# First expert layer: the 26-row tail of the down product in fp32 on four column blocks, and W2's high part made on GpSimd

## The chip, the cores and the metric

The kernel runs on one core of one Trainium2 chip. The metric is device time in microseconds (us) of one launch; lower is better. Three runs of the kernel before took 1910.48, 1913.32 and 1914.53 us, a median of 1913.32 us.

The engines are named as in the profile: PE (TensorE matmuls) with PEld (its weight loads), DVE (VectorE), ACT (ScalarE), POOL (GpSimd) and SP (SyncE, which issues DMAs here).

## The reference, cut to what matters

The network has four attention layers and four feed-forward layers in turn. The change lies in the first feed-forward layer, a mixture of 8 experts, each token going to its two best, each expert taking at most C = 538 rows of 256 numbers:

```python
C = int(round(K * T * CAP_RATIO / E))                       # 538
h = gelu(einsum('ecd,edh->ech', buf, W1) + b1[:, None, :])  # 538 x 256 times 256 x 1024
y = einsum('ech,ehd->ecd', h, W2) + b2[:, None, :]          # 538 x 1024 times 1024 x 256
```

The second line of arithmetic is called the up product below, the third the down product. Both are to be had in about fp32 accuracy.

## The kernel before

The program is written engine by engine: each engine has one function per layer, its instructions run in the order in which they are written, and engines meet at semaphores alone (`wait_ge`, `then_inc`). No scheduler moves anything.

**Split operands.** A fast matmul form takes operands rounded to fewer bits ("rounded" in the profile, type fp32r). Each matrix is therefore split into a high part (a rounded copy, `act_hi`, `act_split_w1`, `act_split_w2`) and a low part (the rest, `dve_lo`, one SCALAR_TENSOR_TENSOR at L918), and a product is the sum of three matmuls: high by high, high by low, low by high.

**One expert.** For expert x, PE does (`pe_ffn0`):
- `pe_up0`: eight blocks f of 128 hidden units. A block is 12 matmuls of 270 columns (two halves of the 540 row slots), into banks 4 and 5 or 6 and 7 in turn. Before it writes a pair of banks again it waits for the Gelu of block f-2.
- `pe_rows` for expert x + 1: ten transposes that turn the next expert's rows, into banks 0, 1 and 2.
- `pe_down0`: five blocks a of rows, four of 128 and a tail of 26. A block is 24 matmuls of 256 columns (8 blocks f by three products), so the tail costs PE the same 24 matmuls as a full block. The blocks go to banks 3, 2, 3, 2, 3 in turn; block a waits for DVE to have taken block a-2 (`s_yd`), except that block 1 waits only for the tail of the turned rows to have left bank 2 (`s_xpd`).

**Around it, for each block f of the up product:** ACT does the Gelu (L1113, 128x540, out of PSUM into `f0_HF`, which has two buffers, so that Gelu f waits for the low part of f-2); the high part of h is made by ACT for even f (L1119) and by DVE for odd f (L1156, a CAST); DVE makes the low part (L918). Behind blocks 1 and 3 ACT makes one half of W2's high part (L915, 128x1024) and DVE the low part (L918, 128x1024).

**After the eighth block** ACT, then DVE, split the next expert's turned rows (three pieces) and its W1 (two halves). Only then does DVE's program come to `f0_Y = PSUM + b2` (L1173), which empties the five down blocks one by one. POOL waits for each and scatters its rows to memory (L1210, an indirect DMA), then makes the row indices of expert x + 2 (L1071).

**Loads.** SP loads the weights of expert x + 2, 2 MB in one DMA, as soon as expert x's W1 and W2 are split, into the buffer that they leave.

Of the kernel before, what the change touches and what calls it, by code (L numbers as in the profile page):

```python
# [92 lines left out]
def build(nc, d, out):  # L93
    with ExitStack() as ctx:
# [64 lines left out]
        s_zsrc, s_zero, s_w0 = sem("zero_tile"), sem("buffers_zeroed"), sems("ffn0_w_in", 2)  # L159
        s_gate, s_bf = sem("gates"), sem("bf16_consts")  # L160
        s_rin, s_rout = sems("rows_in", 4), sems("rows_out", 3)
        s_x, s_bn, s_rs, s_xn = sem("x_tile"), sem("bn_stats"), sem("rstd"), sem("xn_tile")
        s_tp, s_xt = sem("turned"), sem("xt_cols")

# [58 lines left out]
        def sp_begin(e):  # L223
            e.dma_start(X[:, 0:4, :], d["x"][:, 0:4, :]).then_inc(s_xin[0], 16)
            e.dma_start(view(oC, NCST), d["cst"]).then_inc(s_const, 16)
            e.dma_start(ctxT, d["ctxT"]).then_inc(s_const, 16)
            e.dma_start(view(oS, NSML), d["sml"]).then_inc(s_const, 16)
            e.dma_start(X[:, 4:8, :], d["x"][:, 4:8, :]).then_inc(s_xin[1], 16)
            e.dma_start(view(oAW, 2048), d["aw"][0]).then_inc(s_aw[0], 16)
            for g in range(2, 4):  # L230
                e.dma_start(X[:, 4 * g:4 * g + 4, :], d["x"][:, 4 * g:4 * g + 4, :]).then_inc(s_xin[g], 16)
            e.dma_start(view(oAW + 2048, 2048), d["aw"][1]).then_inc(s_aw[1], 16)
            for x in range(2):
                e.dma_start(view(oW + 4096 * x, 4096), d["w0"][x]).then_inc(s_w0[x], 16)
            sp_blank(e)
# [4 lines left out]
        def sp_blank(e):  # L240
            e.wait_ge(s_zsrc, 1)
# [10 lines left out]
        def pool_begin(e):  # L252
            e.memset(view(z_tile, RW), 0.0).then_inc(s_zsrc, 1)
            e.wait_ge(s_const, 48)
            for t in range(NT):
                pool_rstd(e, t + 1, t)
# [44 lines left out]
        s_kv, s_kb, s_vp, s_vz = sem("kv_prod"), sem("kb_ready"), sem("vp_ready"), sem("vp_blank")  # L301
# [76 lines left out]
        def dve_heads(e, L):  # L378
# [14 lines left out]
            e.wait_ge(s_vz, 2 * L + 2)  # L393
# [496 lines left out]
        XP, HP = rview(oXT, 2, 2, CAP + 2), rview(o + 4160, 2, 8, CAP + 2)  # L890
        f0_B2, f0_Y = view(oXT + 2160, 2, 256), view(oXT + 2672, 3, 256)
# [6 lines left out]
        s_xg = sem("rows_blank")  # L898
# [3 lines left out]
        s_dn, s_yd = sem("down_prod"), sem("y_ready")  # L902
        s_f0b = sems("b2_in", 2)
# [16 lines left out]
        def act_split_w1(e, x):  # L920
            e.wait_ge(s_w0[x % 2], 16 * (x // 2 + 1))
            if x:
                e.wait_ge(s_up, 8 * x)
            for k in range(2):
                act_hi(e, W1P[:, 0, k], raw_w1(x, k), s_w1a)

        def dve_split_w1(e, x):
            e.wait_ge(s_w0[x % 2], 16 * (x // 2 + 1))
# [6 lines left out]
        def act_split_w2(e, x, h):  # L935
            if x:
                e.wait_ge(s_dn, 5 * x)
            act_hi(e, parts_w2(h)[0], raw_w2(x, h), s_w2a)

# [12 lines left out]
        def pe_rows(e, x):  # L952
# [11 lines left out]
            if x >= 2:  # L964
                e.wait_ge(s_yd, 5 * (x - 1) - 1)
# [18 lines left out]
        def down_bank(a):  # L984

            return 3 - a % 2

        def pe_down0(e, x):
            e.wait_ge(s_w2d, 2 * x + 2)
            for a in range(5):  # L990
                n = 128 if a < 4 else 26
                bk = down_bank(a)
                if a >= 2:
                    e.wait_ge(s_yd, 5 * x + a - 1)
                elif a == 1 and x < 7:
                    e.wait_ge(s_xpd, 3 * x + 6)
                elif x:
                    e.wait_ge(s_yd, 5 * x - a)
                for f in range(8):
                    if a == 0:  # L1000
                        e.wait_ge(s_hl, 8 * x + f + 1)
                    for i, j in ((0, 0), (0, 1), (1, 0)):
                        m = mm(e, psum[0:n, bk, 0:256], HP[:, i, f, 128 * a:128 * a + n], W2P[:, j, f, :],
                               (f, i, j) == (0, 0, 0), (f, i, j) == (7, 1, 0))
                m.then_inc(s_dn, 1)

# [60 lines left out]
        def pool_ids0(e, x):  # L1067
            e.wait_ge(s_rin[x % 2], 32 * (x // 2 + 1))
            if x == 0:
                e.wait_ge(s_xg, 1)  # L1070
# [3 lines left out]
        def pe_ffn0(e):  # L1074
            pe_ranks0(e, 1)
            pe_ranks0(e, 2)
            pe_rows(e, 0)
# [18 lines left out]
        def act_ffn0(e):  # L1096
# [10 lines left out]
            for x in range(8):  # L1107
                for f in range(8):
                    bk, hf = 4 + 2 * (f % 2), f0_HF[:, f % 2, :]
                    e.wait_ge(s_up, 8 * x + f + 1)  # L1110
                    if 8 * x + f >= 2:
                        e.wait_ge(s_hl, 8 * x + f - 1)
                    e.activation(hf.rearrange("p (c n) -> p c n", c=2), psum[:, bk:bk + 2, 0:270], ACT.Gelu,  # L1113
# [6 lines left out]
                    if f in (1, 3) and x:  # L1120
                        act_split_w2(e, x, f // 2)
                if x < 7:
                    act_rows(e, x + 1)
                    act_split_w1(e, x + 1)

        def dve_ffn0(e):
# [15 lines left out]
            e.memset(f0_Xg[:, :, 4, :], 0.0).then_inc(s_xg, 1)  # L1142
# [53 lines left out]
        def pool_ffn0(e):  # L1196
# [10 lines left out]
            for x in range(8):  # L1207
                for a in range(5):
# [4 lines left out]
                    ny += 1  # L1213
                if x < 6:
                    pool_ids0(e, x + 2)
# [6 lines left out]
        def sp_ffn0(e):  # L1222
            def load_w(x):
                e.wait_ge(s_w1d, 2 * (x - 1))
                e.wait_ge(s_w2d, 2 * (x - 1))
                e.dma_start(view(oW + 4096 * (x % 2), 4096), d["w0"][x]).then_inc(s_w0[x % 2], 16)
# [18 lines left out]
            e.wait_ge(s_xg, 1)  # L1245
# [3 lines left out]
            for x in range(6):  # L1249
# [3 lines left out]
                load_b(x + 2)  # L1253
            e.wait_ge(s_dn, 40)
# [1888 lines left out]
```

## Time and profile before

| | us |
|---|---|
| median of three runs | 1913.32 |
| span of the profiled execution | 1915.2 |
| PE busy in the span | 1641.2 (86%) |
| DVE, ACT, POOL busy | 1092.3, 898.9, 837.6 |
| chain that ended last, PE's share | 64%, of it 60% at L166 |
| chain at L166 in one expert: 216 matmuls | 26.43 |

The page gives the profiled execution by its span alone, from the first instruction to the last; no other time is listed for it. It is 1.9 us over the median and 0.7 us over the slowest of the three runs. The expert stage of this layer lies between 170 and 397 us of the span. All matmuls are issued by one helper at L166, the low parts by another at L918, so that groups by line mix layers: rows are to be read by time and by shape.

### The profile page before, as it was taken

How to read it: one execution, taken by the hardware profiler on the slowest of the kernel's cores; microseconds unless marked ns; L12 is line 12 of the kernel's file. 1: busy time of each engine (PE TensorE's matmuls, PEld its weight loads, DVE VectorE, ACT ScalarE, POOL GpSimd, SP SyncE). 2: the span in 40 equal slices, each digit the busy share in tenths (PEclk: the TensorE clock that was granted, in tenths of full speed). 3: DMA queues.
4: the chain of work that ended last, by engine and by line, in shares of the span. 5: the costliest groups of instructions: out<-in, count | busy, mean ns of one | idle time of the engine just before them, and what ended most of it. 6: DMA issues, size and time to landing. Idle time of an engine off the chain costs nothing.

```text
span 1915.2 us, 26188 instructions
## 1 busy us (share of the span) xinstructions
PE 1641.2 (86%) x9225; PEld 1117.0 (58%) x9225; DVE 1092.3 (57%) x2218; ACT 898.9 (47%) x1454; POOL 837.6 (44%) x754
## 2 busy tenths in 40 slices
PE   5954999969966999965996887999999999997998
PEld 3444999946844333355993665555555654563674
DVE  4762556576967355532446798565656666644335
ACT  2322445513335897823443664555454355431363
POOL 3053211123479454422005464566656666754206
PEclk9776999979987899977998987999999999997999
DMA  9613233030000000062113000000000000012354
GB/s 363 225 55 110 79 138 132 21 118 1 1 22 1 1 6 6 7 279 83 51 43 107 1 1 33 1 1 1 1 0 1 1 1 1 0 54 92 125 166 132
DMA packets 61879, 117.76 MB, mean 61 GB/s; under 512 B 7247, under 2 KB 50499, under 8 KB 59064
## 3 DMA queue, kind: packets, MB, share of 16 engines
q1 hardware_dynamic: 53688, 95.90, 14.3%
q0 software_dynamic: 8064, 20.19, 3.2%
q8 instruction: 77, 1.26, 0.3%
q14 instruction: 50, 0.41, 0.1%
HBM read 72.26 MB, written 44.89 MB: 61 GB/s over the span
## 4 chain that ended last, share of the span: by engine, by line
PE 64%; DVE 14%; POOL 9%; issue 4%; DMA 4%; ACT 4%; SPq 0%; POOLq 0%; DVEq 0%; ACTq 0%
PE psum L166 60%; POOL arena L1839 3%; DMA arena<-xb 2%; DVE arena L2401 2%; POOL arena L870 2%; DVE rounded L2330 2%; DVE arena L1736 1%; POOL xb L1057 1%; DVE arena L171 1%; POOL arena L1856 1%; DVE arena L2473 1%; PE psum L682 1%; DVE arena L1968 1%; ACT arena L1607 1%; DVE arena L187 1%
## 5 line engine op out<-in xcount | busy, mean ns | idle before, releaser
L166 PE MATMUL psum<-arena 128*128 (+16 forms) x5084 | 1029.4, 438 | 115.3 <-DVE arena L1717 20.0
L166 PEld LDWEIGHTS psum<-arena 128*128 128x128 f32 (+4 forms) x5084 | 587.4, 175 | 451.7 <-issue 289.8
L166 PE MATMUL psum<-rounded 128*128 128x256 f32 (+9 forms) x3072 | 535.2, 340 | 5.8 <-ACT rounded L1572 1.4
L166 PEld LDWEIGHTS psum<-rounded 128*128 128x128 f32 (+5 forms) x3072 | 406.5, 186 | 143.0 <-issue 56.1
L2501 POOL TENSOR_TENSOR arena<-arena 128x1024 f32<-128x1024 f32 (+1 forms) x111 | 263.2, 2371 | 130.9 <-ACT arena L2451 127.3
L2401 DVE TENSOR_REDUCE arena<-psum 128x1 f32<-128x512 f32 x256 | 163.9, 682 | 98.3 <-PE psum L166 96.7
L2451 ACT ACTIVATE arena<-psum 128x1024 f32<-128x1024 f32 x144 | 147.4, 1025 | 147.6 <-PE psum L166 146.9
L1607 ACT ACTIVATE arena<-psum,arena 128x1024 f32<-128x1024 f32 x128 | 134.7, 1117 | 24.0 <-PE psum L166 22.5
L870 POOL DMA_INDIRECT arena<-yb,arena x48 | 45.9, 957 | 211.1 <-DMA yb<-arena 197.6
L1210 POOL DMA_INDIRECT yt<-arena x40 | 39.8, 996 | 182.8 <-DVE arena L1173 177.3
L918 DVE SCALAR_TENSOR_TENSOR rounded<-arena,rounded 128x540 fp32r<-128x540 f32 (+1 forms) x96 | 81.9, 886 | 33.4 <-ACT rounded L1119 32.3
L1113 ACT ACTIVATE arena<-psum,arena 128x540 f32<-128x540 f32 x64 | 45.5, 711 | 107.5 <-PE psum L166 104.8
L176 POOL TENSOR_SCALAR arena<-arena 128x1 f32<-128x1 f32 x89 | 22.0, 247 | 148.0 <-DVE arena L172 121.0
L1859 POOL TENSOR_TENSOR arena<-arena 128x256 f32<-128x256 f32 (+1 forms) x48 | 44.2, 935 | 90.8 <-ACT arena L1607 90.8
L2330 DVE SCALAR_TENSOR_TENSOR rounded<-psum,rounded 64x512 fp32r<-64x512 f32 (+1 forms) x80 | 47.6, 595 | 61.5 <-ACT rounded L2308 32.6
L1814 DVE SCALAR_TENSOR_TENSOR arena<-psum,arena 128x128 f32<-128x128 f32 x92 | 26.0, 345 | 74.1 <-PE psum L166 74.1
L214 ACT ACTIVATE arena<-psum 128x512 f32<-128x512 f32 x48 | 27.6, 596 | 83.5 <-PE psum L206 83.4
L2473 DVE RECIPROCAL arena<-arena 128x128 f32<-128x128 f32 x64 | 58.9, 936 | 11.9 <-ACT arena L2317 11.6
L206 PE MATMUL psum<-arena 128*128 128x128 f32 x192 | 31.9, 304 | 31.1 <-DVE arena L187 29.2
L2498 POOL TENSOR_TENSOR arena<-arena 128x1024 f32<-128x1024 f32 x16 | 38.1, 2381 | 44.9 <-ACT arena L2451 44.9
L1839 POOL TENSOR_TENSOR arena<-arena 128x20 f32<-128x20 f32 x16 | 56.9, 3556 | 1.3
L171 DVE BATCH_NORM_STATS2 arena<-arena 128x6 f32<-128x256 f32 x128 | 54.3, 424 | 3.3
(266 smaller groups left out, 1905.5 us busy)
## 6 DMA issues: line engine op xcount, KB each, us to landing
arena<-in_w SPq DMA_DIRECT2D x8, 2048.0 KB, 8.4
arena<-xb SPq DMA_DIRECT2D x70, 128.0 KB, 2.3
yb<-arena SPq DMA_DIRECT2D x70, 128.0 KB, 1.8
arena<-in_w1u SPq DMA_DIRECT2D x4, 2048.0 KB, 14.5
xb<-arena SPq DMA_DIRECT2D x3, 2048.0 KB, 16.0
xb<-arena SPq DMA_DIRECT2D x2, 2064.0 KB, 31.5
arena<-xb SPq DMA_DIRECT2D x8, 516.0 KB
yt<-arena SPq DMA_DIRECT2D x2, 2048.0 KB, 15.6
```

What stands on the lines that cost most here:

```text
L166: return e.matmul(o, l, r, start=start, stop=stop, skip_group_check=True)
L171: settle(e, dve, e.bn_stats(ST[:, t, :], src(t)))
L870: e.indirect_dma_start(dst, None, buf, bass.IndirectOffsetOnAxis(idx[:, col:col + 1], 0)).then_inc(s_gth[s], 16)
L918: e.scalar_tensor_tensor(out=dst, in0=src, scalar=1.0, in1=hi, op0=ALU.mult, op1=ALU.subtract).then_inc(sig, 1)
L1113: e.activation(hf.rearrange("p (c n) -> p c n", c=2), psum[:, bk:bk + 2, 0:270], ACT.Gelu, bias=sml("b1c")[:, 8 * x + f:8 * x + f + 1]).th ...
L1607: e.activation(PT[:, u % 3, 2 * h:2 * h + 2, :], psum[:, bk:bk + 2, :], ACT.Exp, bias=NBD[:, 0:1]).then_inc(s_ae, 1)
L1839: e.tensor_tensor(RSH[:, t % 4, :], RSH[:, t % 4, :], cst("nhalf")[:, 0:1].broadcast_to([128, 20]), ALU.pow).then_inc(s_rh, 1)
L2330: e.scalar_tensor_tensor(out=lo, in0=psum[r, bk, 0:64 if (kind, c) == ("k", 2) else 512], scalar=1.0, in1=hi, op0=ALU.mult, op1=ALU.subtra ...
L2401: m = e.tensor_reduce(x3_MX[:, t, a, c:c + 1], psum[:, bk, :], AX.X, ALU.max)
L2451: e.activation(x3_P[0:rows, g % 4].rearrange("p a n -> p (a n)"), psum[0:rows, bk:bk + 2, :].rearrange("p a n -> p (a n)"), ACT.Exp, scale ...
L2473: e.reciprocal(x3_RC[:, 128 * i:128 * i + 128], x3_SM[:, 128 * i:128 * i + 128]).then_inc(s_rc3, 1)
L2501: m = e.tensor_tensor(ac, ac, x3_P[0:rows, g % 4], ALU.add)
```

## The change

- **Tail.** The 26-row tail is no longer part of the loop of five blocks. ACT does a second Gelu for each f (128x28, straight from PSUM) into a small fp32 tile `f0_TH`, padded with zeros to 32 columns. `pe_tail0`, issued after block 0, does eight fp32 matmuls with the unsplit W2: for n = 0, 1 and column block c = 0 to 3, hidden block f = 2c + n, output to partitions 32c to 32c + 31 of bank 2. So each column block holds a quarter of the sum. ACT copies the four quarters to SBUF (`f0_TP`), and after block 3 one fp32 matmul with a constant selector `f0_TS` (128x32, four stacked identities) adds them, into bank 2.
- **Banks.** Blocks 0 to 3 and the selector go to banks 3, 3, 2, 3, 2. Block 1 now waits for DVE to have taken block 0; block 2 for ACT's copy of the quarters; block 3 for block 1; the selector for block 2.
- **W2's high part** for experts 1 to 7 is made by POOL (two CASTs of 128x1024), in POOL's program after the five scatters of the expert before; ACT makes it for expert 0 alone.
- **Loads.** W1 and W2 come in DMAs of their own, 1 MB each, and W2's waits until the tail no longer reads the raw W2.
- Two semaphores are merged with others to make room for two new ones.

```diff
         def pool_split_w2(e, x, h):
+            e.wait_ge(s_w0[x % 2], 32 * (x // 2 + 1))
+            e.wait_ge(s_dn, 5 * x)
+            e.tensor_copy(parts_w2(h)[0], raw_w2(x, h)).then_inc(s_w2a, 1)
...
         def down_bank(a):
-            return 3 - a % 2
+            return (3, 3, 2, 3, 2)[a]
 
         def pe_down0(e, x):
             e.wait_ge(s_w2d, 2 * x + 2)
-            for a in range(5):
-                n = 128 if a < 4 else 26
+            for a in range(4):
                 bk = down_bank(a)
-                if a >= 2:
-                    e.wait_ge(s_yd, 5 * x + a - 1)
-                elif a == 1 and x < 7:
-                    e.wait_ge(s_xpd, 3 * x + 6)
-                elif x:
-                    e.wait_ge(s_yd, 5 * x - a)
+                if a == 0 and x:
+                    e.wait_ge(s_yd, 5 * x - 1)
+                elif a == 2:
+                    e.wait_ge(s_tk, x + 1)
+                elif a:
+                    e.wait_ge(s_yd, 5 * x + a - a // 2)
...
                 m.then_inc(s_dn, 1)
+                if a == 0:
+                    pe_tail0(e, x)
+            e.wait_ge(s_yd, 5 * x + 3)
+            mm(e, psum[0:32, down_bank(4), 0:256], f0_TS, f0_TP, True, True).then_inc(s_dn, 1)
+
+        def pe_tail0(e, x):
+            if x < 7:
+                e.wait_ge(s_xpd, 3 * x + 6)
+            if x:
+                e.wait_ge(s_yd, 5 * x)
+            for n in range(2):
+                for c in range(4):
+                    m = mm(e, psum[32 * c:32 * c + 32, 2, 0:256], f0_TH[:, 2 * c + n, :],
+                           view(oW + 4096 * (x % 2) + 2048, 8, 256)[:, 2 * c + n, :], n == 0, n == 1)
+            m.then_inc(s_tl, 1)
...
+                    e.activation(f0_TH[:, f, 0:CAP - 510], psum[:, bk + 1, 242:270], ACT.Gelu,
+                                 bias=sml("b1c")[:, 8 * x + f:8 * x + f + 1])
                     e.activation(hf.rearrange("p (c n) -> p c n", c=2), psum[:, bk:bk + 2, 0:270], ACT.Gelu,
...
-                    if f in (1, 3) and x:
-                        act_split_w2(e, x, f // 2)
                 if x < 7:
                     act_rows(e, x + 1)
                     act_split_w1(e, x + 1)
+                e.wait_ge(s_tl, x + 1)
+                if x:
+                    e.wait_ge(s_dn, 5 * x)
+                e.activation(f0_TP, psum[:, 2, 0:256], ACT.Copy).then_inc(s_tk, 1)
...
                     ny += 1
+                if x < 7:
+                    for h in range(2):
+                        pool_split_w2(e, x + 1, h)
                 if x < 6:
                     pool_ids0(e, x + 2)
```

On PE, at the end of the first expert (from the last three matmuls of block 0 to the next expert's up product), the order before is this; `y_ready` is `s_yd`, `rows_lo` is `s_xpd`:

```order
L166 MATMUL psum<-rounded 128x256 [waits h_lo]
L166 MATMUL psum<-rounded 128x256 x2
L166 MATMUL psum<-rounded 128x256 [waits rows_lo]
L166 MATMUL psum<-rounded 128x256 x23
L166 MATMUL psum<-rounded 128x256 [waits y_ready]
L166 MATMUL psum<-rounded 128x256 x23
L166 MATMUL psum<-rounded 26x256 [waits y_ready]
L166 MATMUL psum<-rounded 26x256 x23
L166 MATMUL psum<-rounded 128x270 [waits gelu,w1_lo,rows_lo]
```

and with the change, where `tail_kept` is ACT's copy of the quarters:

```order
L167 MATMUL psum<-rounded 128x256 [waits h_lo]
L167 MATMUL psum<-rounded 128x256 x2
L167 MATMUL psum<-arena 32x256 [waits rows_lo]
L167 MATMUL psum<-arena 32x256 x7
L167 MATMUL psum<-rounded 128x256 [waits y_ready]
L167 MATMUL psum<-rounded 128x256 x23
L167 MATMUL psum<-rounded 128x256 [waits tail_kept]
L167 MATMUL psum<-rounded 128x256 x23
L167 MATMUL psum<-arena 32x256 [waits y_ready]
L167 MATMUL psum<-rounded 128x270 [waits gelu,w1_lo,rows_lo]
```

Twenty-four matmuls at the end have become eight after block 0 and one after block 3, and block 1, which waited for the rows' low part, now waits for `y_ready`, that is for DVE's addition of block 0.

On POOL, from the last scatters of rows to the experts into the stage, the order before (L1210 scatters an expert's five result tiles, L1071 makes row indices):

```order
L1071 TENSOR_SCALAR arena<-arena 128x5 [waits rows_blank,rows_in0]
L1071 TENSOR_SCALAR arena<-arena 128x5 [waits pool,rows_in1]
L1210 DMA yt<-arena 4096x256 [waits pool,y_ready]
L1210 DMA yt<-arena 4096x256 [waits y_ready] x4
L1071 TENSOR_SCALAR arena<-arena 128x5 [waits rows_in0]
L1210 DMA yt<-arena 4096x256 [waits pool,y_ready]
```

and with the change, where L1238 and L1092 are the same two lines and L944 is the new CAST of W2:

```order
L1092 TENSOR_SCALAR arena<-arena 128x5 [waits bf16_consts_and_rows_blank,rows_in0]
L1092 TENSOR_SCALAR arena<-arena 128x5 [waits pool,rows_in1]
L1238 DMA yt<-arena 4096x256 [waits pool,y_ready]
L1238 DMA yt<-arena 4096x256 [waits y_ready] x4
L944 CAST rounded<-arena 128x1024 [waits down_prod,ffn0_w_in1] x2
L1092 TENSOR_SCALAR arena<-arena 128x5 [waits rows_in0]
L1238 DMA yt<-arena 4096x256 [waits pool,y_ready]
```

The two CASTs stand behind all five scatters of an expert and behind the end of its down product (`down_prod`), and ahead of the row indices.

## Rows read from the trace of the kernel before

**Rows 1.** Chain of waits in order of time: start us, us, what.

```profile
244.10 26.43 PE psum L166 x216
...
270.53 0.87 PE psum L959 x8
...
271.63 26.43 PE psum L166 x216
...
394.88 0.42 DVE arena L1173
```

**Rows 2.** Busy time by stretch: PE, PEld, DVE, ACT, POOL, clock, DMA.

```profile
251.00:278.00 27.00, 27.00 (x224) 26.46 (x223) 15.25 (x24) 12.97 (x19) 4.97 (x6) 1.00 0.35 124
```

**Rows 3.** Timeline, end of an expert: start us, us, engine, line, idle before.

```profile
255.70 0.42 DVE L1173 TENSOR_TENSOR arena<-psum,arena 128x256 f32<-128x256 f32 x1 [2.42 <-PE psum L166]
...
258.50 0.41 DVE L1173 TENSOR_TENSOR arena<-psum,arena 26x256 f32<-26x256 f32 x1 [2.37 <-PE psum L166]
...
259.68 0.98 POOL L1210 DMA_INDIRECT yt<-arena  x1 [1.80 <-DVE arena L1173]
...
260.68 0.26 POOL L1071 TENSOR_SCALAR arena<-arena 128x5 uint32<-128x5 f32 x1
```

**Rows 4.** Timeline of PE in a later attention layer, 700 to 703 us.

```profile
699.76 0.64 PE L166 MATMUL psum<-arena 128*32 128x256 f32 x8
700.33 0.93 PE L166 MATMUL psum<-rounded 48*128 48x512 f32 x4
```

**Rows 5.** Timeline of the next expert, DVE and the start of its down product.

```profile
261.45 0.72 DVE L918 SCALAR_TENSOR_TENSOR rounded<-arena,rounded 128x540 fp32r<-128x540 f32 x1 [2.54 <-ACT rounded L1119]
...
262.27 0.44 DVE L1156 CAST rounded<-arena 128x540 fp32r<-128x540 f32 x1
262.74 2.49 DVE L918 SCALAR_TENSOR_TENSOR rounded<-arena,rounded 128x540 fp32r<-128x540 f32 x3
...
270.49 0.72 DVE L918 SCALAR_TENSOR_TENSOR rounded<-arena,rounded 128x540 fp32r<-128x540 f32 x1 [0.99 <-ACT rounded L1119]
...
271.31 0.44 DVE L1156 CAST rounded<-arena 128x540 fp32r<-128x540 f32 x1
...
271.56 8.67 PE L166 MATMUL psum<-rounded 128*128 128x256 f32 x71
...
273.74 2.36 DVE L918 SCALAR_TENSOR_TENSOR rounded<-arena,rounded 128x1024 fp32r<-128x1024 f32 x2
276.01 0.42 DVE L1173 TENSOR_TENSOR arena<-psum,arena 128x256 f32<-128x256 f32 x1
```

**Rows 6.** Groups by line and shape, ACT: count, busy us, mean ns, idle before.

```profile
L915 ACT ACTIVATE rounded<-arena 128x1024 fp32r<-128x1024 f32 x32 | 32.8, 1062 | 0.0
...
L915 ACT ACTIVATE rounded<-psum 128x56 fp32r<-128x56 f32 x8 | 1.8, 226 | 0.0
```

**Rows 7.** Timeline of POOL before the stage: scatters with nothing to wait for.

```profile
139.33 0.98 POOL L1057 DMA_INDIRECT xb<-arena  x1 [0.30 <-issue]
140.62 0.98 POOL L1057 DMA_INDIRECT xb<-arena  x1 [0.30 <-issue]
```

**Rows 8.** Groups by line and shape, POOL, of the fourth attention layer.

```profile
L2630 POOL TENSOR_SCALAR rounded<-arena 64x1088 fp32r<-64x1088 f32 x2 | 5.9, 2970 | 5.2 <-ACT arena L2567 5.1
L2631 POOL CAST rounded<-arena 1x1088 fp32r<-1x1088 f32 x2 | 2.2, 1084 | 0.1
```

**Rows 9.** Timeline of POOL in the third attention layer, 1066 to 1069 us.

```profile
1066.60 1.90 POOL L2041 TENSOR_TENSOR arena<-arena 128x1024 f32<-128x1024 f32 x1 [6.92 <-DVE arena L1970]
```

**Rows 10.** Timeline of DVE in the same stretch.

```profile
1067.37 1.42 DVE L1997 SCALAR_TENSOR_TENSOR arena<-arena 128x256 f32<-128x256 f32 x1
```

**Rows 11.** Timeline of DVE, 1090 to 1092 us, the same line.

```profile
1091.06 0.49 DVE L1997 SCALAR_TENSOR_TENSOR arena<-arena 128x256 f32<-128x256 f32 x1
```

**Rows 12.** Timeline of PE, 570 to 592 us: one of five like it.

```profile
581.36 1.53 PE L166 MATMUL psum<-arena 128*128 128x384 f32 x4 [1.90 <-DVE arena L1717]
```

**Rows 13.** Timeline of PE, 770 to 780 us.

```profile
775.40 2.55 PE L166 MATMUL psum<-arena 128*128 128x512 f32 x10 [2.27 <-DVE arena L1663]
```

**Rows 14.** Busy time by stretch, columns as in Rows 2.

```profile
571.00:591.00 20.00, 11.10 (x58) 7.81 (x59) 16.96 (x48) 11.87 (x30) 19.33 (x13) 1.00 0.00 0
592.00:598.00 6.00, 5.34 (x17) 3.64 (x16) 4.13 (x11) 2.52 (x6) 5.75 (x6) 0.50 0.00 0
...
776.00:779.00 3.00, 3.00 (x14) 0.70 (x12) 1.20 (x2) 0.97 (x2) 0.00 (x0) 0.50 0.00 0
```

More of the change, by code:

```diff
@@ L163, in build @@
         s_tp, s_xt = sem("turned"), sem("xt_cols")
+        s_vz = sem("zero_tile_and_vp_blank")
         def mm(e, o, l, r, start, stop):
@@ L233, in sp_begin @@
             for x in range(2):
-                e.dma_start(view(oW + 4096 * x, 4096), d["w0"][x]).then_inc(s_w0[x], 16)
+                for h in (slice(0, 2048), slice(2048, 4096)):
+                    e.dma_start(view(oW + 4096 * x, 4096)[:, h], d["w0"][x][:, h]).then_inc(s_w0[x], 16)
             sp_blank(e)
@@ L252, in pool_begin @@
         def pool_begin(e):
-            e.memset(view(z_tile, RW), 0.0).then_inc(s_zsrc, 1)
+            e.memset(view(z_tile, RW), 0.0).then_inc(s_vz, 1)
             e.wait_ge(s_const, 48)
@@ L392, in dve_heads @@
             e.wait_ge(s_kv, 2 * L + 2)
-            e.wait_ge(s_vz, 2 * L + 2)
+            e.wait_ge(s_vz, 2 * L + 3)
             for h in range(2):
@@ L902, in build @@
         s_dn, s_yd = sem("down_prod"), sem("y_ready")
+        s_tl, s_tk = sem("tail_quarters"), sem("tail_kept")
         s_f0b = sems("b2_in", 2)
@@ L927, in dve_split_w1 @@
         def dve_split_w1(e, x):
-            e.wait_ge(s_w0[x % 2], 16 * (x // 2 + 1))
+            e.wait_ge(s_w0[x % 2], 32 * (x // 2 + 1))
             if x:
@@ L964, in pe_rows @@
             if x >= 2:
-                e.wait_ge(s_yd, 5 * (x - 1) - 1)
+                e.wait_ge(s_yd, 5 * (x - 1))
             for k in range(2):
@@ L1069, in pool_ids0 @@
             if x == 0:
-                e.wait_ge(s_xg, 1)
+                e.wait_ge(s_bf, 2)
             settle(e, pool, e.tensor_scalar(f0_ID[:, x, :], f0_Xg[:, x % 2, :, 256], float(GONE), None, ALU.add))
@@ L1076, in pe_ffn0 @@
             pe_ranks0(e, 2)
+            e.wait_ge(s_bf, 2)
             pe_rows(e, 0)
@@ L1141, in dve_ffn0 @@
                                                   in1=f0_WI.rearrange("p (k t) -> p k t", k=2), op0=ALU.mult, op1=ALU.mult))
-            e.memset(f0_Xg[:, :, 4, :], 0.0).then_inc(s_xg, 1)
+            e.memset(f0_TH[:, :, CAP - 510:32], 0.0)
+            e.tensor_reduce(f0_TS, ident.rearrange("p (c r) -> p r c", c=4), AX.X, ALU.add)
+            e.memset(f0_Xg[:, :, 4, :], 0.0).then_inc(s_bf, 1)
             e.wait_ge(s_zero, N_ZERO)
@@ L1224, in load_w, with load_w2 @@
                 e.wait_ge(s_w1d, 2 * (x - 1))
+                e.dma_start(view(oW + 4096 * (x % 2), 2048), d["w0"][x][:, 0:2048]).then_inc(s_w0[x % 2], 16)
+            def load_w2(x):
                 e.wait_ge(s_w2d, 2 * (x - 1))
-                e.dma_start(view(oW + 4096 * (x % 2), 4096), d["w0"][x]).then_inc(s_w0[x % 2], 16)
+                e.wait_ge(s_tl, x - 1)
+                e.dma_start(view(oW + 4096 * (x % 2) + 2048, 2048), d["w0"][x][:, 2048:4096]).then_inc(s_w0[x % 2], 16)
             def load_rows(x):
@@ L1244, in sp_ffn0 @@
             e.wait_ge(s_sct[1], 16 * 16)
-            e.wait_ge(s_xg, 1)
+            e.wait_ge(s_bf, 2)
             for x in range(2):
@@ L1253, in sp_ffn0 @@
                 load_b(x + 2)
+                load_w2(x + 2)
             e.wait_ge(s_dn, 40)
```

17 lines of the change are left out of this document (8 added, 9 removed).

## The prediction

> **What bounds the kernel now.** I read the slices first, then the chain of waits in order of time, the stretch table, and at last the timeline of one expert. In the slices the stage from 170 to 397 us is one of the few where PE is busy in every tenth. The chain shows why: it is PE's own queue, expert after expert, 216 matmuls at L166 (the down product of one expert and the up product of the next) and ten transposes, and it comes round every 27.53 us (271.63 - 244.10) [rows 1]. In the stretch table PE is busy 27.00 us of 27.00 at a granted clock of 1.00 (the upper level, 2.4 GHz), while DVE has 15.25, ACT 12.97 and POOL 4.97 [rows 2]. So here PE time counts one for one, and the other engines count only where PE is made to wait for them. The reader should see in the timeline that the tail is a full block in PE's time: DVE takes the fourth block at 255.70 and the tail at 258.50, 2.80 us later [rows 3].
>
> **PE's own work.** Removed: 24 matmuls, 2.80 us an expert. Added: eight fp32 matmuls over four column blocks, and the selector. A group of the same shape stands in a later layer: eight 128*32 matmuls of 256 columns start at 699.76 and the next, of another shape, at 700.33, so 0.57 us with the turn to the next shape in it [rows 4]; the column blocks run side by side. The selector is one matmul of that shape: at least half of this, 0.29, at most all, 0.57; I take 0.40, since it has two turns of shape around it. By PE's work alone an expert gains 2.80 - 0.57 - 0.40 = 1.83 us, eight of them 14.6.
>
> **The new wait.** Block 1 used to go to bank 2 and waited for nothing late. Now it goes to bank 3, just filled by block 0, and waits for DVE to empty it. DVE's program has the next expert's rows and W1 ahead of that. In the timeline block 0 begins at 271.56 and is through 2.80 later, at 274.36; DVE's two W1 pieces run from 273.74, and block 0 is emptied from 276.01 to 276.43 [rows 5]. Before, this was hidden behind block 1, since only block 2 waited for it. The new tail covers 0.57 of it, and PE then stands until 276.43. I add 0.15 for the small Gelus and 0.1 for PE to start again (bounds 0 and 0.2). A small Gelu is nearest to a 128x56 ACTIVATE, 226 ns [rows 6]; two of them lie ahead of the last Gelu, so 0 to 0.45, and I take 0.15 because ACT has some idle time there. Block 1 then starts at 276.68 instead of 274.36, 2.32 later. With the selector and without the old tail: 2.32 + 0.40 - 2.80 = -0.1 us for an expert. The wait alone takes back the whole of the 1.83. What waits behind block 1 on PE is everything: blocks 2 and 3, the selector, the next up product.
>
> The other new waits cost nothing: block 2's for ACT's copy and the selector's for block 2 have a whole block, 2.8 us, over them. Nor do the loads: W2 of expert x + 2 is asked for at the end of expert x, a period ahead of its use.
>
> **W2's high part on POOL.** Taken from ACT: two ACTIVATEs of 1.06 us an expert [rows 6], which PE did not wait for; worth nothing. Put on POOL: two CASTs. The nearest row is a CAST of 1088 elements to fp32r, 1.08 us, though on one partition; a TENSOR_SCALAR to fp32r on 64 partitions took 2.97 [rows 8]. For 1024 elements the bounds are 1.0 and 2.8; I take 1.05, the same operation.
>
> When do they run? Before, POOL is free for its next operation 2.18 us after DVE begins to take the tail (260.68 - 258.50) [rows 3]. With the change the selector's result follows block 3 by 0.4 us, so its scatter queues behind block 3's; scatters that wait for nothing follow each other by 1.29 us (140.62 - 139.33) [rows 7]. That makes 3.5 us after block 3 is taken, some 3.2 after the next up product starts. DVE's first low part of the next expert starts at 261.45, 2.95 after the tail is taken [rows 5]. So the CASTs fall exactly where DVE gets busy, not into its 2.54 us of idle time ahead.
>
> Does that hurt DVE? In a later layer POOL runs a TENSOR_TENSOR from 1066.60 to 1068.50 [rows 9]; DVE's SCALAR_TENSOR_TENSOR on two SBUF operands, started at 1067.37 inside it, takes 1.42 us and ends at 1068.79, just after POOL [rows 10]; the same instruction takes 0.49 otherwise [rows 11]. DVE stood still until POOL was done. The low parts of h and W2 are that kind of instruction. The Trainium skill, page "SBUF — State Buffer", section "Who interferes with whom", says that DVE and GpSimd share one pair of ports, and that whichever starts first keeps it for its whole instruction when DVE reads two SBUF operands, or copies in a two-port mode, and GpSimd reads SBUF; the trace agrees in the rows just named. By that rule every DVE instruction between the CASTs is shut out and the forecast below stands; without it the first rival's sum does.
>
> From 261.45 to 271.31 DVE is busy but for 0.99 us before the seventh low part and two gaps of 0.1 [rows 5], 1.19 together. Two CASTs and the row indices (0.26 [rows 3]) add 2.36. So DVE comes to its last CAST at least 1.17 late; at most 2.36, if nothing is made up, because late low parts hold back the Gelus and these PE's up blocks. I take 1.4, near the lower end, since most of the idle time is one piece that can be used up. This passes straight through to block 1: 2.32 - 0.15 + 1.4 = 3.57 later, so 3.57 + 0.40 - 2.80 = +1.17 us for an expert.
>
> **The sum.** Expert 0 has no CAST of POOL's in its up product: -0.1. Experts 1 to 6: +1.17 each, +7.0. Expert 7 has no next rows or W1, so block 0 is emptied within the tail and PE keeps its 1.83; but its last scatter follows block 3's by 1.29 instead of 2.80, which after the 0.57 of the tail leaves about 0.9 at the end of the stage (394.88 [rows 1]), and its up product is late by about 1.0 from the CASTs: +0.1. Together +7.0: 1922.2 us on the profiled execution's 1915.2, and on the median, 1.9 below that span, 1913.3 + 7.0, about 1920. With every bound at its low end an expert costs 2.32 - 0.25 + 1.17 + 0.29 - 2.80 = +0.73, six of them 4.4; with all at the high end (2.36, 0.45, 0.2, 0.57) +2.4, 14.4. Own range 1917 to 1928.
>
> **Rivals.** *POOL's CASTs do not hold DVE up*, because they fall into gaps or do not shut out these instructions. For it: DVE is idle 43% of the stage [rows 2]. Against: rows 9 to 11, and the time at which they start. Then experts 0 to 6 are worth -0.1 each and the last -0.9: 1913.3 - 1.6, about 1912; not slower. *The whole PE gain arrives*: that needs DVE to empty block 0 within 0.6 us of its end; the timeline has 2.07 between (276.43 - 274.36). 1913.3 - 14.6 = 1899. *The clock falls.* PE would now stand some 2.0 us in each of experts 1 to 6 (block 0 about 1 us late from the up product, tail through at 275.9, block 1 at 277.9). In the trace waits of 1.90 us pass five times at a clock of 1.00, and after the fifth there are 6 us at 0.50, the lower level, 1.2 GHz; after one of 2.27 there are 3 at 0.50 [rows 12 to 14]. It decides if the new waits end like that of 2.27 and not like the first four of 1.90. Three us at half the clock lose 1.5; six times that is 9.0 more: 1929. *POOL's CAST is slow*, 2.8 instead of 1.05: 3.5 more for DVE, six times: 1941; against it, the row of the same operation.
>
> **How the numbers follow.** The forecast has a chance of 0.52, POOL's CASTs unfelt 0.20, the whole gain 0.07, the clock 0.14, a slow CAST 0.07. The measurement tells 0.2%, 3.8 us, from no change: slower is 0.71 (the forecast but for 0.02, the clock, the slow CAST), within it 0.18 (0.16 of the unfelt CASTs, and 0.02), faster 0.11. The range takes in the first rival's 1912 less 2 and the clock: 1910 to 1929.
>
> **What would show it.** In the profile after: PE idle before block 1, put down to DVE's addition, in seven of eight experts, 1.5 us in the first and about 2 in those after; DVE low parts and CASTs of over 1 us beside POOL's two CASTs; POOL's CASTs at 1.05 us where they wait for nothing; a period of 28.7 us for experts 1 to 6 instead of 27.5; eight tail matmuls in 0.6 us. I am wrong if block 1 starts right after the tail, if the CASTs run while DVE is idle, or if DVE's instructions keep their 0.72 us beside them.

## The result and the profile after

| | before | after |
|---|---|---|
| median of 12 runs, us | 1911.30 | 1916.41 |
| lowest to highest, us | 1907.48 to 1914.65 | 1913.18 to 1918.95 |
| ratio, 95% interval | | 1.0024 (1.0015 to 1.0034) |
| expert stage, first transpose to the last scatter's start, us | 226.35 | 231.75 |
| one expert (up product to up product), experts 1 to 6, us | 27.54 | 28.38 |

The change makes the kernel slower, by 0.24%: 4.6 us on the 1913.3 of the prediction, 2.9 to 6.5 by the interval. The profiled execution of after has a span of 1911.4 us, 3.8 below that of before. That is no contradiction: the twelve runs before lie 7.2 us apart from lowest to highest, and the other layers take their share of that, so two single spans don't put kernels in order. The stage does, since it repeats: in both traces its experts 1 to 6 agree within 0.05 us. It is 5.40 us longer. The start times of matmuls in this and the next sections are taken from the trace of each kernel. An up product is measured from the start of its first matmul to the start of its last, an expert from one up product's first matmul to the next one's. Experts and blocks are counted from 0.

The chain of waits of after in order of time (start us, us, what) answers to [rows 1]. Before, it was PE's own queue; now it leaves PE twice in an expert:

```profile
250.90 11.06 PE psum L167 x86
...
262.16 0.71 ACT arena L1137
...
262.90 0.66 ACT rounded L1143
...
263.59 2.25 DVE rounded L921
...
266.10 0.71 ACT arena L1137
266.86 6.31 PE psum L167 x48
...
277.67 1.22 DVE rounded L921
278.89 0.35 DVE arena L1201
279.28 11.05 PE psum L167 x86
```

It comes round every 28.38 us (279.28 - 250.90) against 27.53. The stretch table (PE, PEld, DVE, ACT, POOL, clock, DMA) answers to [rows 2]: in 28 us PE is busy 26.88, no longer the whole stretch, and POOL has 8.05 where it had 4.97 of 27. The clock stays at 1.00, as everywhere between 178.6 and 407.3 us.

```profile
251.00:279.00 28.00, 26.88 (x220) 25.12 (x220) 16.25 (x24) 12.72 (x26) 8.05 (x8) 1.00 0.34 121
```

The list of PE's waits in the stage (who waits for whom: total us, times, longest) has two entries that come back, the first in experts 0 to 6, the second in experts 1 to 7:

```profile
PE psum L167 <- DVE arena L1201: 7.0, 7, 1.0
PE psum L167 <- ACT arena L1137: 2.8, 7, 0.4
```

Inside the stage no wait of PE's is put down to a DMA, so the loads in two pieces cost it nothing.

The first of the two waits stands before block 1 of the down product. The timeline of after (start us, us, engine, line, operation, idle before and who ended it) shows it in expert 3, and is the counterpart of [rows 5]:

```profile
271.96 0.72 DVE L921 SCALAR_TENSOR_TENSOR rounded<-arena,rounded 128x540 fp32r<-128x540 f32 x1
273.29 0.72 DVE L921 SCALAR_TENSOR_TENSOR rounded<-arena,rounded 128x540 fp32r<-128x540 f32 x1 [0.61 <-ACT rounded L1143]
...
274.18 3.10 PE L167 MATMUL psum<-rounded 128*128 128x256 f32 x24
277.21 1.07 PE L167 MATMUL psum<-arena 128*32 128x256 f32 x16
279.28 1.92 PE L167 MATMUL psum<-rounded 128*128 128x256 f32 x14 [1.00 <-DVE arena L1201]
...
276.54 2.35 DVE L921 SCALAR_TENSOR_TENSOR rounded<-arena,rounded 128x1024 fp32r<-128x1024 f32 x2
278.81 0.42 DVE L1201 TENSOR_TENSOR arena<-psum,arena 128x256 f32<-128x256 f32 x1
```

Block 0 starts at 274.18, the tail at 277.21, and PE stands until DVE, busy with the next expert's W1, has emptied block 0 at 279.23. Block 1 starts 5.10 us after block 0 (279.28 - 274.18), where it used to be 2.94 (by the trace of before, 271.56 to 274.50). The eight fp32 matmuls of the tail are 16 records.

The second wait is in the up product. The timeline at its start:

```profile
260.17 6.29 PE L167 MATMUL psum<-rounded 128*128 128x270 f32 x48
260.93 0.99 POOL L1238 DMA_INDIRECT yt<-arena  x1 [1.85 <-DVE arena L1201]
262.22 0.98 POOL L1238 DMA_INDIRECT yt<-arena  x1 [0.30 <-issue]
263.18 2.06 POOL L944 CAST rounded<-arena 128x1024 fp32r<-128x1024 f32 x2
263.59 2.24 DVE L921 SCALAR_TENSOR_TENSOR rounded<-arena,rounded 128x540 fp32r<-128x540 f32 x1 [2.90 <-ACT rounded L1143]
265.17 1.04 POOL L1092 TENSOR_SCALAR arena<-arena 128x5 uint32<-128x5 f32 x1
266.10 0.70 ACT L1137 ACTIVATE arena<-psum,arena 128x540 f32<-128x540 f32 x1
266.86 6.29 PE L167 MATMUL psum<-rounded 128*128 128x270 f32 x48 [0.40 <-ACT arena L1137]
```

Read it as a chain. POOL casts from 263.18 to 265.24. DVE's first low part starts inside that, at 263.59, and takes 2.24 us instead of 0.72. Gelu 2 waits for that low part, because `f0_HF` has two buffers; the small Gelu of the same block, which stands in front of it, waits too and takes 0.18 us of its own (265.92 to 266.10). Gelu 2 ends at 266.80; PE waits for Gelu 2 to start block 4. PE idles 0.40 by the record; 0.68 lie between the start of the matmul before and that of block 4's first, where neighbours are 0.12 apart.

The Trainium skill, page "SBUF — State Buffer", section "Who interferes with whom", has the rule cited in the prediction: of a DVE instruction that reads two SBUF operands and a GpSimd one that reads SBUF, the second to come stands still. The trace agrees, 2.24 against 0.72 us.

The difference per expert, experts 1 to 6, by start times:

| part | predicted | measured |
|---|---|---|
| block 0's first matmul to block 3's last (11.36 to 13.60), longer by the wait before block 1 | +3.57 | +2.24 |
| old tail gone, selector added (end of block 3 to the next up product: 2.91 to 0.76) | -2.40 | -2.15 |
| up product longer (11.94 to 12.68) | 0 | +0.74 |
| sum | +1.17 | +0.83 |

Of the 2.24, 2.16 lie ahead of block 1 (2.94 to 5.10).

### The profile page after: what moved, and what is told of

Read it like the earlier page. It is cut to its first block, busy times and chain, and to the rows that moved or that the text cites. A ratio compares the mean times of both kernels' runs of the same rounds, so it can differ in the third digit from the quotient of the medians.

```text
span 1911.4 us, 26202 instructions
## 1 busy us (share of the span) xinstructions
PE 1625.8 (85%) x9177; PEld 1098.6 (57%) x9177; DVE 1100.7 (58%) x2220; ACT 897.3 (47%) x1512; POOL 856.4 (45%) x768
## 4 chain that ended last, share of the span: by engine, by line
PE 61%; DVE 17%; POOL 8%; ACT 5%; issue 5%; DMA 4%; SPq 0%; POOLq 0%; DVEq 0%; ACTq 0%
PE psum L167 56%; POOL arena L1875 2%; DVE rounded L921 2%; DMA arena<-xb 2%; DVE arena L2437 2%; DVE rounded L2366 2%; POOL arena L872 2%; DVE arena L1772 1%; POOL xb L1078 1%; DVE arena L172 1%; POOL arena L1892 1%; PE psum L207 1%; DVE arena L2509 1%; PE psum L684 1%; ACT arena L1137 1%
## 5 line engine op out<-in xcount | busy, mean ns | idle before, releaser
L167 PE MATMUL psum<-arena 128*128 128x128 f32 (+14 forms) x5228 | 1036.7, 434 | 117.2 <-DVE arena L1753 22.3
L167 PEld LDWEIGHTS psum<-arena 128*128 128x128 f32 (+5 forms) x5228 | 589.9, 172 | 454.0 <-issue 289.2
L167 PE MATMUL psum<-rounded 128*128 128x270 f32 (+7 forms) x2880 | 515.5, 343 | 15.7 <-DVE arena L1201 7.0
L167 PEld LDWEIGHTS psum<-rounded 128*128 128x128 f32 (+3 forms) x2880 | 386.1, 191 | 156.6 <-issue 57.6
L1238 POOL DMA_INDIRECT yt<-arena x40 | 40.2, 1006 | 170.0 <-DVE arena L1201 167.5
L921 DVE SCALAR_TENSOR_TENSOR rounded<-arena,rounded 128x540 fp32r<-128x540 f32 (+1 forms) x96 | 92.4, 996 | 33.4 <-ACT rounded L1143 32.3
L1135 ACT ACTIVATE arena<-psum,arena 128x28 f32<-128x28 f32 x64 | 17.9, 280 | 105.0 <-PE psum L167 90.5
```

The source lines that it names most:

```text
L167: return e.matmul(o, l, r, start=start, stop=stop, skip_group_check=True)
L921: e.scalar_tensor_tensor(out=dst, in0=src, scalar=1.0, in1=hi, op0=ALU.mult, op1=ALU.subtract).then_inc(sig, 1)
```

## The experiments

The theory is the prediction's: the bank wait takes back PE's gain and POOL's CASTs add the loss. Rival A says that the fp32 matmuls are themselves as dear as the old tail; rival B gives the whole loss to the CASTs and holds the bank wait to be covered. Where a diff is cut, the waits that go with it are told in words. Stage, expert and up product are read from each kernel's trace. The times are medians of twelve runs, of six for bank1_and_act and bank1_casts_earlier and of four for wait_alone; the ratios are to the kernel before, run beside it on the same chip.

| kernel | stage, us | expert, us | up product, us | median, us | ratio, 95% |
|---|---|---|---|---|---|
| w2_on_act | 227.57 | 27.84 | 12.15 | 1913.15 | 1.0005 (0.9993 to 1.0016) |
| pool_w2_only | 226.32 | 27.54 | 11.94 | 1912.07 | 1.0001 (0.9985 to 1.0017) |
| block1_own_bank | 224.31 | 27.30 | 12.68 | 1908.89 | 0.9991 (0.9980 to 1.0002) |
| bank1_and_act | 220.38 | 26.76 | 12.15 | 1903.20 | 0.9960 (0.9944 to 0.9976) |
| casts_earlier | 227.46 | 27.73 | 12.03 | 1909.63 | 0.9997 (0.9984 to 1.0010) |
| early_add | 220.46 | 26.77 | 12.15 | 1905.01 | 0.9964 (0.9951 to 0.9976) |
| wait_alone | 248.03 | 29.61 or 31.1 | 11.94 | 1930.10 | 1.0101 (1.0078 to 1.0125) |
| tail_twice | 232.78 | 28.39 | 12.68 | 1916.03 | 1.0030 (1.0017 to 1.0043) |
| bank1_casts_earlier | 219.54 | 26.64 | 12.03 | 1902.18 | 0.9957 (0.9941 to 0.9973) |

**w2_on_act: the change without POOL's CASTs.**

```diff
+                    if f in (1, 3) and x:
+                        act_split_w2(e, x, f // 2)
...
-                if x < 7:
-                    for h in range(2):
-                        pool_split_w2(e, x + 1, h)
```

ACT's call also waits for the end of the expert before's down product (`s_dn`).

> The changed kernel with W2's high part back on ACT; tail, selector and banks stay. Theory (two losses: block 1 waits for DVE's addition of block 0, and POOL's CASTs shut DVE out): DVE is on time again, PE still stands about 1.2 us before block 1 in experts 0 to 6, the Gelu wait of 0.4 us and the 2.24 us low parts are gone; about as fast as the kernel before, -1.5 to +1.5 us. Rival A (the fp32 tail with its quarters, Gelus and selector is itself as dear as 24 fast matmuls): +4 to +5 us, as with the whole change. Rival B (POOL's CASTs are the whole loss, the wait before block 1 is harmless): -8 us or more.

The time is where the theory put it. PE's wait for Gelu 2 is gone from its list, the one before block 1 is the same to a hundredth, and so is DVE's part in it (first the list of waits, then the timeline of PE and DVE):

```profile
PE psum L167 <- DVE arena L1205: 7.0, 7, 1.0
```

```profile
261.98 0.72 DVE L921 SCALAR_TENSOR_TENSOR rounded<-arena,rounded 128x540 fp32r<-128x540 f32 x1 [2.90 <-ACT rounded L1145]
...
272.04 3.10 PE L167 MATMUL psum<-rounded 128*128 128x256 f32 x24
...
276.67 0.42 DVE L1205 TENSOR_TENSOR arena<-psum,arena 128x256 f32<-128x256 f32 x1
```

DVE takes block 0 at 276.67 - 272.04 = 4.63 us after PE began it; with the CASTs it was 278.81 - 274.18 = 4.63 as well. So the CASTs cost 0.54 an expert (28.38 - 27.84), all of it in the up product (12.68 - 12.15), and nothing at block 1. Rival B would have left the stage at or under before's 226.35; it is 1.22 above.

**pool_w2_only: the kernel before with its W2 moved to POOL.** ACT's two calls go, and POOL gets two CASTs behind the five scatters.

```diff
-                    if f in (1, 3) and x:
-                        act_split_w2(e, x, f // 2)
...
+                if x < 7:
+                    for h in range(2):
+                        pool_split_w2(e, x + 1, h)
```

> The kernel before with W2's high part on POOL and nothing else of the change: old tail, old banks. Theory: POOL's CASTs still hold one or more of DVE's low parts to over 1.5 us, PE waits 0.3 to 0.5 us for a Gelu in each of experts 1 to 7 and up to 0.3 us for the late addition of block 0 before block 2: +2 to +5 us. Rival A: 0. Rival B: the whole of the change's loss with the PE gain not there, +10 us or more.

A miss: the stage is unchanged, and PE has no wait in it. The timeline shows that the lock is there all the same:

```profile
260.85 2.04 POOL L943 CAST rounded<-arena 128x1024 fp32r<-128x1024 f32 x2
...
261.64 1.84 DVE L918 SCALAR_TENSOR_TENSOR rounded<-arena,rounded 128x540 fp32r<-128x540 f32 x1 [2.54 <-ACT rounded L1124]
...
263.57 0.71 ACT L1118 ACTIVATE arena<-psum,arena 128x540 f32<-128x540 f32 x1 [1.14 <-DVE rounded L918]
```

The CASTs begin 0.79 us before DVE's low part, against 0.41 in the change, so the low part is held for less, 1.84 against 2.24 us. Counted from the up product's first matmul, Gelu 2 ends at 5.79 (264.28 - 258.49) and block 4 starts at 6.04, as in before; in the change Gelu 2 ends at 6.63 (266.80 - 260.17). Being held costs nothing as long as it stays within that slack, which the theory had not counted. DVE's own lateness, 0.94 at its first CAST, is gone at its last one, which starts 13.01 us after the up product as in before: its idle time took up all of it, and none reaches the down product. By this the two CASTs would cost 0.54 an expert in the change because of the time at which they start beside DVE; casts_earlier tests that.

**block1_own_bank: block 1 to bank 1, free by then, so that it doesn't wait for block 0.** Block 1 waits for the turned rows to have left bank 1, block 3 for block 1.

```diff
-            return (3, 3, 2, 3, 2)[a]
+            return (3, 1, 2, 3, 2)[a]
```

> The changed kernel with block 1 in bank 1, which the turned rows have left, instead of bank 3: block 1 no longer waits for DVE's addition of block 0; W2's high part stays on POOL. Theory: the stop before block 1 (1.0 us idle, 1.4 from matmul to matmul) goes in seven experts, the Gelu wait of 0.4 us stays: 6 to 8 us less than the changed kernel, 1.5 to 3.5 less than the kernel before. Rival A: no more than 1 us off the changed kernel, since what takes the time is the tail itself. Rival B: no more than 1 us off the changed kernel, since the CASTs stay.

Block 1 now follows the tail without a wait (timeline of PE), and the one wait left in the list is that for Gelu 2:

```profile
246.30 1.07 PE L167 MATMUL psum<-arena 128*32 128x256 f32 x16
247.30 7.96 PE L167 MATMUL psum<-rounded 128*128 128x256 f32 x65
```

```profile
PE psum L167 <- ACT arena L1139: 2.7, 7, 0.4
```

Against after an expert gains 1.08 (28.38 - 27.30), and the ratio comes down from 1.0024 to 0.9991, as expected. The bank alone is worth 7.44 us of stage (231.75 - 224.31). Both rivals, which gave it no more than 1 us, are refuted. Against before the stage is 2.04 shorter, but the interval of the times just takes in no change.

**bank1_and_act: both undone.** It has the edits of the first and the third experiment.

> Both undone at once: block 1 in bank 1 and W2's high part on ACT; the fp32 tail and its selector stay. Theory: nothing stands in PE's way in the down product; an expert gains 2.80 for the old tail, less about 1.0 for the new one and 0.6 for the selector, 1.2 us; eight times 9 us, less about 0.5 for the last two scatters that follow each other: -7 to -9.5 us against the kernel before. Rival A: +2 to +5. Rival B: the same as theory, but then the kernel with W2 on ACT alone is as fast as this one.

The chain in the stage is PE's alone once more:

```profile
214.88 0.23 PE psum L975 x2
215.11 25.65 PE psum L167 x210
240.76 0.87 PE psum L967 x8
```

The period is 26.76 us, 0.78 under before's 27.54, and the list has no PE wait left in the stage. The time is within what was expected, the gain of an expert below the expected 1.2. So of the 1.83 that the prediction gave PE's own work, 0.78 is there. The rest is the fp32 work being dearer: the tail takes 1.09 instead of 0.57 (1.21 lie between the last matmul of block 0 and the first of block 1 where nothing is waited for, 0.12 between neighbours without a tail), and the selector 0.64 (0.76 - 0.12); 0.21 lies in the up product (12.15 against 11.94). By the start times of its matmuls this is two gaps. Its second matmul comes 0.23 after the first instead of 0.125, in every kernel with the selector ahead of it: 0.10. Block 6's first two matmuls are late by 0.12 together, in the kernels where ACT makes W2's high part and the small Gelus as well: ACT's second half of W2 (1.06 us) stands ahead of Gelu 4, which block 6 waits for. With W2's high part on POOL (bank1_casts_earlier) this second gap is gone. 2.80 - 1.09 - 0.64 - 0.21 is 0.86, near the 0.78. Rival A is refuted: the new pieces are cheaper than the 2.80 us they replace.

**casts_earlier: POOL's CASTs ahead of the fifth scatter.**

```diff
                 for a in range(5):
+                    if a == 4 and x < 7:
+                        for h in range(2):
+                            pool_split_w2(e, x + 1, h)
...
-                if x < 7:
-                    for h in range(2):
-                        pool_split_w2(e, x + 1, h)
```

The CASTs wait for block 3 of the down product (`5 * x - 1` in place of `5 * x`), after which no matmul reads W2's split parts.

> The changed kernel with POOL's two CASTs ahead of the fifth scatter of an expert instead of behind it (they wait for the four full blocks, not for the selector). Theory now: what costs is not that POOL makes W2's high part but when: behind the queued fifth scatter the CASTs start 3.0 us after the up product starts and hold DVE's first low part 1.5 us; 1.3 us earlier they run mostly while DVE is idle. The 0.68 us gap before the fifth up block goes, an up product takes 12.15 instead of 12.68 us, seven times: 3.5 to 4 us less than the changed kernel, within 2 us of the kernel before. Rival (DVE and POOL share something whenever both are at work): no change, or less than 1 us.

Timelines of POOL and DVE:

```profile
260.05 2.05 POOL L944 CAST rounded<-arena 128x1024 fp32r<-128x1024 f32 x2
262.26 1.29 POOL L1241 DMA_INDIRECT yt<-arena  x1 [0.16 <-issue]
...
261.73 0.95 DVE L921 SCALAR_TENSOR_TENSOR rounded<-arena,rounded 128x540 fp32r<-128x540 f32 x1 [2.89 <-ACT rounded L1143]
```

The CASTs end at 262.10, 0.37 into the low part, which takes 0.95. The wait for Gelu 2 is gone and the up product is 12.03, less than the expected 12.15; the stage gains 4.29 on the changed kernel's, a little over the expected 3.5 to 4. The same operations on the same engine cost 0.65 an expert less (28.38 - 27.73), for starting 1.7 us ahead of the low part (261.73 - 260.05) instead of 0.4. The rival is refuted.

**early_add: W2 on ACT, bank 3 kept, but DVE empties block 0 before it splits W1.**

```diff
                 if x < 7:
                     dve_rows(e, x + 1)
+                add(0)
+                if x < 7:
                     dve_split_w1(e, x + 1)
-                for a in range(5):
+                for a in range(1, 5):
+                    add(a)
```

W2's high part goes back to ACT as in w2_on_act.

> W2's high part on ACT, banks as in the changed kernel, but DVE adds block 0 ahead of the next expert's W1 pieces instead of behind them. Theory: the wait before block 1 is only DVE's order; block 0 is emptied within the tail, the gap from block 0 to block 1 falls from 2.28 to 1.2 us as with a bank of its own, and the W1 pieces, 0.4 to 1 us later, are in time for the up product: as fast as the kernel with both undone, -5 to -9 us against the kernel before. Rival: the W1 pieces come late and PE waits at the up product instead: no gain over W2 on ACT alone.

DVE takes block 0 at 272.66 and W1 behind it (timeline of DVE):

```profile
272.66 0.42 DVE L1203 TENSOR_TENSOR arena<-psum,arena 128x256 f32<-128x256 f32 x1 [0.69 <-PE psum L167]
273.00 2.35 DVE L921 SCALAR_TENSOR_TENSOR rounded<-arena,rounded 128x1024 fp32r<-128x1024 f32 x2
```

The list has no PE wait left in the stage, and stage and period are those of bank1_and_act within 0.1 us. So it isn't the bank as such: it is the order in DVE's program that makes the bank late.

**wait_alone: the kernel before, old tail and all, with the change's banks.**

```diff
-            return 3 - a % 2
+            return (3, 3, 2, 3, 2)[a]
```

The waits follow the banks.

> The kernel before, old tail and W2 on ACT, with the banks 3, 3, 2, 3, 2 alone: block 1 waits for DVE's addition of block 0 with no tail in between. Theory: PE stands about 2.1 us (from 274.4 to 276.5 in the third expert) in each of experts 0 to 6 and 0.6 us in the last: +14 to +16 us. Were the wait harmless: 0.

PE's wait before block 1 is 1.82 us by the record, for nothing covers any of it. What it does to the clock is seen in the stretch table, which has 0.50 right behind it and 1.00 after (timeline row first, then the table):

```profile
284.80 5.48 PE L166 MATMUL psum<-rounded 128*128 128x256 f32 x31 [1.82 <-DVE arena L1175]
```

```profile
280.00:284.00 4.00, 2.98 (x24) 2.77 (x24) 3.97 (x7) 2.56 (x5) 0.00 (x0) 1.00 0.94 380
285.40:288.70 3.30, 3.30 (x18) 3.30 (x17) 0.00 (x0) 0.00 (x0) 1.06 (x1) 0.50 0.11 40
289.00:292.00 3.00, 3.00 (x27) 3.00 (x26) 0.42 (x1) 0.00 (x0) 0.99 (x1) 1.00 0.03 5
```

Two of the experts 1 to 6 take 29.61 us, 2.07 more than before: the wait. Four take 31.1, 1.5 more again: 3.3 us at the lower level, 1.2 GHz, lose half their length. Both kinds of expert have the same wait of 1.82, so what chooses between them isn't shown. The stage is 21.7 us longer than before's, by its last scatter:

```profile
418.03 0.98 POOL L1212 DMA_INDIRECT yt<-arena  x1 [1.81 <-DVE arena L1175]
```

The waits account for the expected 14 to 16 of it, four stretches at the lower clock for some 6 more. The median is 19.8 us longer (14.9 to 23.9 by the interval). So the wait is far from harmless, and the theory's amount was too small because it had no term for the clock.

**tail_twice: the eight fp32 matmuls done twice.**

```diff
-            for n in range(2):
+            for n in (0, 1, 0, 1):
```

> The changed kernel with the eight tail matmuls issued twice over, the second pass writing the same sums. Theory: PE stands 1.07 us behind the tail in experts 0 to 6, and a second tail of 0.86 us fits into that; only expert 7 pays: 0 to +2 us against the changed kernel, the gap from block 0 to block 1 still 2.28 us. Rival A (the tail's own time is on the path): +6 to +7 us.

Twice the records, 32, in 1.93 us, and block 1 starts where it did (timeline of PE):

```profile
248.11 1.93 PE L167 MATMUL psum<-arena 128*32 128x256 f32 x32
250.18 8.79 PE L167 MATMUL psum<-rounded 128*128 128x256 f32 x72
```

The period is the same, 28.39. Of the stage's 1.03 us, 0.87 fall into expert 7, which has no such wait to hide them; its block 1 starts 4.79 after block 0 instead of 3.92. In the change the tail's time is free in experts 0 to 6, and rival A's 6 to 7 us are refuted.

**bank1_casts_earlier: the best of these, the third and the fifth edit together.**

> Block 1 in bank 1 and POOL's CASTs ahead of the fifth scatter, so that W2's high part stays on POOL and neither loss is left. Theory: the gap from block 0 to block 1 is 1.2 us, an up product takes 12.03 us as with the earlier CASTs alone, the period is 26.65 us and the stage some 6.5 us shorter than before: -6 to -9 us, the same as or 1 us better than with W2 on ACT. Rival (POOL and DVE disturb each other wherever PE does not wait anyway): over 1 us slower than with W2 on ACT and block 1 in bank 1.

Timelines of PE and POOL:

```profile
240.93 3.09 PE L167 MATMUL psum<-rounded 128*128 128x256 f32 x24
243.95 1.07 PE L167 MATMUL psum<-arena 128*32 128x256 f32 x16
244.95 8.78 PE L167 MATMUL psum<-rounded 128*128 128x256 f32 x72
253.67 0.62 PE L167 MATMUL psum<-arena 128*32 128x256 f32 x2
254.22 4.03 PE L167 MATMUL psum<-rounded 128*128 128x270 f32 x30
...
255.94 2.05 POOL L944 CAST rounded<-arena 128x1024 fp32r<-128x1024 f32 x2
```

The list has no PE wait left in the stage; the period is 26.64 and the stage 6.81 us shorter than before's. At 0.9957 (0.9941 to 0.9973) it beats both kernels. With POOL's CASTs out of DVE's way it is also 0.12 an expert under bank1_and_act, where ACT makes W2's high part and block 6 of the up product is late by that much; the times of the two can't be told apart.

## Why the prediction was right, and where it was not

The direction and the mechanism that takes back the gain were right, and 1916.4 lies in the range of 1910 to 1929, but just under the forecast's own range of 1917 to 1928. The sum was +7.0; the stage shows +5.4 and the times +4.6. That it came so near is in part luck: of the terms of an expert's +1.17, the CASTs were 0.86 too dear, and PE's own work was 0.45 too cheap.

- *The new wait: right.* Block 1 was to start 5.12 us after block 0 without CASTs (276.68 - 271.56 in its own figures); it starts 5.10 after, in experts 0 to 6. The start before was misread: a block was taken as 2.80, but block 1 came 2.94 after block 0, so it is later by 2.16 and not by 2.32. The small Gelus, taken at 0.15, show as 4.63 in place of 4.45 until DVE takes block 0: 0.18. Expert 0 came out 0.03 shorter, for a predicted 0.1.
- *POOL's CASTs: price, time and lock right.* 14 of them took 1.049 to 1.075 us (taken: 1.05). They start 3.0 us after the up product (taken: 3.2), and the low part beside them takes 2.24. One row of them all, by line (shortest, median and longest, in ns):

```profile
L944 POOL CAST rounded<-arena x14: 1049/1058/1075, 206.4 to 377.7; 128x1024 fp32r<-128x1024 f32 x14
```

- *"This passes straight through to block 1": wrong.* This is the step that failed. The sum let DVE be late by 1.4 while PE kept its time, and charged 1.4 to the wait before block 1. That wait is 1.0 in each of experts 0 to 6, with CASTs and without. The CASTs and the row indices did not add 2.36 to DVE's work either: the low part grew by 1.52 (2.24 - 0.72), since the CASTs had begun 0.41 ahead of it, and the row indices ran while DVE was at work, 1.04 us long. DVE's first CAST was 1.34 late against w2_on_act, counted from the up product's start, its last one 0.54. The idle time took up the rest, 0.61 of it still being left before the seventh low part. The 0.54 is PE's own lateness: the late low part held Gelu 2, Gelu 2 held block 4 of the up product, and DVE's last pieces wait for the last Gelus, which follow PE. So at block 1 the two stood as before. In pool_w2_only, where Gelu 2 is in time, DVE's last CAST is not late at all. The cost is 0.54 instead of 1.4. The prediction had named this path ("late low parts hold back the Gelus") but used it only for its upper bound; it is a branch that lowers the cost.
- *PE's own work: mis-sized.* The tail takes 1.09 instead of 0.57, because each fp32 matmul is two records and [rows 4] was read as eight matmuls: it was four. In both places four records start within 0.02 us of each other, and the next four 0.24 later. The selector costs some 0.64 instead of 0.40. Only the selector is felt (tail_twice), about +0.25 an expert, and the up product has 0.21 more that the sum didn't have. These two make up for part of the CASTs' too high price.
- *The Trainium skill*, page "FP8 and Floating Point Precision", section "TensorE Precision Notes", says that true fp32 takes four passes through the array. An estimate by it: two rounds of four column blocks side by side, four passes each, at 0.117 us a pass (2.80 over 24 matmuls of the same 256 columns), 0.94 us for the tail; the trace has 1.07 for its 16 records. Weighed ahead of the prediction it would have pointed to a wrong count in [rows 4].
- *Expert 7*: +0.4 for a predicted +0.1.
- *The rivals.* CASTs unfelt: refuted in the change, true of pool_w2_only. The whole gain: it isn't there to be had, 0.78 an expert is. Slow CAST: refuted. The clock: it did not fall in the stage, where 1.0 us of idle time is left instead of the 2.0 foreseen, because the dearer tail covers part of the wait and PE is late with DVE; with 1.82 (wait_alone) it fell after four of seven waits. The case for this rival was misread: the five waits at a clock of 1.00 behind [rows 12] are not all of 1.90 but 2.29, 1.65, 1.90, 1.89 and 1.89, and one of 1.89 at 563.13, just ahead of them, was followed by 3 us at 0.50. A wait of 2.29 passed where one of 2.27 did not, so their length alone does not tell which will be followed by the lower clock (timeline of PE before):

```profile
572.57 1.53 PE L166 MATMUL psum<-arena 128*128 128x384 f32 x4 [2.29 <-DVE arena L1717]
```

- *The upper bound.* It names 0.45 for the small Gelus, but its +2.4 is 2.07 + 0.2 + 2.36 + 0.57 - 2.80, without them; with them it is +2.85 an expert, and the forecast's own range would end at about 1930.

## What to carry to other kernels

Before shortening a piece of the critical engine's queue, ask what that piece was covering: here a bank emptied late by DVE lay hidden behind the next block, and the shorter tail paid nothing until the block had another bank or DVE another order. Before work is put on an idle engine, look at what the engine that it holds up (here DVE) does at that time, and not at idle shares: the same two CASTs cost 0.54 us an expert or nearly nothing, by where they stand among the scatters. When a side engine becomes late, follow the lateness along every path to the critical engine, since the first one that bites can delay both and so take the load off the later ones.

## What the runs showed of the hardware that was not expected

- Two CASTs on POOL, one behind the other, keep DVE's two-operand instruction out through both: it didn't get in between them (2.24 us, ended 0.6 after the second). The other way round, POOL's index operation of 0.26 us took 1.04 beside DVE, and a scatter of 0.98 took 1.29.
- An fp32 matmul into 32 columns is recorded twice, and four of them over four column blocks run side by side: 16 records in 1.07 us, 32 in 1.93, so 0.86 for eight matmuls and about 0.2 for the turns of shape and the end.
- Waits of 1.82 us were followed by some 3.3 us at a granted clock of 0.50 in experts 2, 3, 4 and 6 and not in 0, 1 and 5, in the same place of the same loop; the changed kernel's waits of 1.0 were not.
- The second matmul behind the selector, and behind a wait of PE's in the up product, starts 0.23 after the first instead of 0.125.
